# Attention over graph edges: the drops' product as four of 32 columns before the messages, factors first in ScalarE's turn

## What is computed

```python
def gatv2_layer(x, Ws, bs, Wd, bd, attn, src, dst):
    hs = (x @ Ws + bs).reshape(N, H, HD)
    hd = (x @ Wd + bd).reshape(N, H, HD)
    hs_e = hs[src]
    e = jax.nn.leaky_relu(hs_e + hd[dst], SLOPE)
    logits = jnp.einsum('ehd,hd->eh', e, attn)
    m = jax.ops.segment_max(logits, dst, num_segments=N)
    ex = jnp.exp(logits - m[dst])
    s = jax.ops.segment_sum(ex, dst, num_segments=N)
    alpha = ex / s[dst]
    out = jax.ops.segment_sum(alpha[..., None] * hs_e, dst, num_segments=N)
    return jax.nn.elu(out).reshape(N, DM)
```

## Time and profile before

| what | value |
|---|---|
| median of 3 runs | 2284.72 us (2283.73 to 2286.36) |
| span of the profiled execution | 2282.6 us |
| granted TensorE clock, mean | 0.974 of full speed |
| TensorE products | 2141.9 us, 94% |
| TensorE weight loads | 1718.3 us, 75% |
| VectorE | 1671.1 us, 73% |
| ScalarE | 1120.7 us, 49% |
| GpSimd | 770.2 us, 34% |

### The profile page before, as it was taken

The page is one execution under the profiler, slowest core; times in us unless marked ns, Lnnn a source line. Parts: engine busy times, 40 slices in busy tenths (PEclk is TensorE's granted clock), DMA queues, the critical chain, the costliest instruction groups (busy, mean ns, idle before and its releaser), DMA issues. The chain is left out here.

```text
span 2282.6 us, 91572 instructions
## 1 busy us (share of the span) xinstructions
PE 2141.9 (94%) x32341; PEld 1718.3 (75%) x32342; DVE 1671.1 (73%) x4413; ACT 1120.7 (49%) x2757; POOL 770.2 (34%) x798
## 2 busy tenths in 40 slices
PE   5999999998999999999996899899999999999578
PEld 3665555555899999999995556589999999999467
DVE  5224997343888888888887674488888888888873
ACT  1101210023666666666664324466666666666463
POOL 0000001111555555555552001255555555554000
PEclk9999999999999999999998899999999999999789
DMA  5000224333788888888874024488888888887301
GB/s 190 0 1 11 76 97 101 106 121 86 239 251 250 252 250 248 247 256 252 251 249 135 23 85 131 131 244 252 251 249 252 251 252 251 250 249 225 133 22 47
DMA packets 139236, 397.61 MB, mean 174 GB/s; under 512 B 21704, under 2 KB 76267, under 8 KB 139123
## 3 DMA queue, kind: packets, MB, share of 16 engines
q0 software_dynamic: 59584, 298.64, 43.0%
q1 hardware_dynamic: 76525, 90.41, 12.6%
q10 hardware_dynamic: 3044, 7.45, 1.1%
HBM read 368.18 MB, written 16.78 MB: 169 GB/s over the span
## 5 line engine op out<-in xcount | busy, mean ns | idle before, releaser
L498 ACT ACTIVATE at_relu<-at_turned,ah_attn_size 128x512 f32<-128x512 f32 x1092 | 717.9, 694 | 432.0 <-PE at_turned L557 430.6
L479 POOL DMA_INDIRECT at_rows<-table,ah_index x360 | 361.3, 1004 | 295.3 <-DVE ah_index L681 104.1
L479 POOL DMA_INDIRECT ah_room<-table,ah_index x352 | 351.5, 998 | 291.1 <-DVE ah_index L681 122.4
L555 PE MATMUL at_turned<-ah_place,dst_rows 96*128 96x128 bf16 x2208 | 401.1, 223 | 19.3 <-ACTq L533 9.6
L557 PE MATMUL at_turned<-ident,ah_room 128*128 128x128 f32 x2208 | 416.4, 279 | 0.0
L557 PE MATMUL at_turned<-ident,at_rows 128*128 128x128 f32 x2160 | 403.6, 277 | 0.5 <-issue 0.4
L555 PE MATMUL at_turned<-at_place,dst_rows 96*128 96x128 bf16 x2160 | 388.9, 222 | 0.0
L677 DVE SCALAR_TENSOR_TENSOR sums<-sums,at_factor,at_total 128x97 f32 x1456 | 344.0, 310 | 9.0 <-issue 5.1
L557 PEld LDWEIGHTS at_turned<-ident,ah_room 128*128 128x128 f32 x2208 | 317.7, 144 | 24.8
L557 PEld LDWEIGHTS at_turned<-ident,at_rows 128*128 128x128 f32 x2160 | 308.0, 143 | 23.2 <-issue 0.6
L667 DVE TENSOR_TENSOR at_spread<-at_lined,at_weight 128x1024 f32<-128x1024 f32 x182 | 223.0, 1225 | 131.4 <-ACT at_weight L508 118.0
(11 more groups left out here) (318 smaller groups left out, 3195.8 us busy)
## 6 DMA issues: line engine op xcount, KB each, us to landing
at_flags<-run_flags SPq DMA_DIRECT2D x182, 64.0 KB
dst_rows<-pr_parts SPq DMA_DIRECT2D x76, 144.0 KB, 2.5
ah_place<-local_rows SPq DMA_DIRECT2D x92, 96.0 KB
at_place<-local_rows SPq DMA_DIRECT2D x90, 96.0 KB
table<-ah_room SPq DMA_DIRECT2D x20, 400.0 KB, 2.4
ah_room<-table,ah_index POOLq DMA_INDIRECT x368
at_rows<-table,ah_index POOLq DMA_INDIRECT x360
mx_w<-in_L_mix_W_qkv SPq DMA_DIRECT2D x2, 2304.0 KB, 19.3
```

Source lines behind the costliest of these rows:

```text
L479: pool.indirect_dma_start(rows[b][:, j, :], None, table, bass.IndirectOffsetOnAxis(index[b][:, j:j + 1], 0)).then_inc(gathered[b], 16)
L498: act.activation(relu[c][:], turned[chunk(b, c)][:], ACT.Relu, scale=attn_size[:, c:c + 1]).then_inc(bent, 1)
L555: pe.matmul(into, dst_rows[:, bass.ds(at[j], 1), c * P:(c + 1) * P].rearrange("p o d -> p (o d)"), place[b][:, j * P:(j + 1) * P], start=T ...
```

## The change

- `sum_drops` becomes four products of 32 columns instead of one of 128: each takes 32 columns of `head_rows` and writes 32 partitions. The result goes to the bank `back`, behind its first 128 columns, and no longer to `heads`. It now waits for the weights of the macro as well, since they are read from the same bank.
- On TensorE it moves from between chunks 4 and 5 to the front of the next turn, directly before the messages of the same macro.
- On ScalarE `factors` moves from in front of bend 5 to the front of the next turn, which is directly behind bend 5. Both programs get one more turn at the end for it.
- `sum_heads` no longer waits for the factors; the last product into `back` (after the loop) does.

```diff
                 def factors(m, b):
                     act.wait_ge(turned_back, 2 * m + 2)
                     for j in range(G):
-                        act.activation(factor[b % 2][:, j, :], heads[:, P + j * HH:P + (j + 1) * HH], ACT.Exp,
+                        act.activation(factor[b % 2][:, j, :], back[:, P + j * HH:P + (j + 1) * HH], ACT.Exp,
                                        scale=first_dst[:, bass.ds(m * G + j, 1)]).then_inc(weights_ready, 1)
-                def slot(turn, head, first=False, fresh=False):
+                def slot(turn, head, message, first=False):
+                    if message:
+                        factors(message[0], message[1])
                     if turn:
                         bend(turn[0], turn[1], 0, first)
...
                         bend(turn[0], turn[1], 4, first)
-                    if head:
-                        factors(head[0], head[1])
-                    if turn:
                         bend(turn[0], turn[1], 5, first)
...
                 with act.Fori(0, LOOPS) as i:
                     for b in range(UNROLL):
-                        slot(macro(i, b + 2), macro(i, b + 1))
+                        slot(macro(i, b + 2), macro(i, b + 1), macro(i, b))
...
                 def sum_heads(m, b):
                     pe.wait_ge(scanned, m * SCANS + SCANS)
-                    pe.wait_ge(weights_ready, m * EXPS + EXPS)
...
                 def sum_drops(m):
                     pe.wait_ge(dropped, m + 1)
-                    pe.matmul(heads[:, P:P + G * HH], head_rows[:], drop[:], start=True, stop=True).then_inc(turned_back, 1)
+                    pe.wait_ge(weights_ready, m * EXPS + (EXPS + 1))
+                    for q in range(HM):
+                        last = pe.matmul(back[q * S:(q + 1) * S, P:P + G * HH], head_rows[:, q * S:(q + 1) * S], drop[:], start=True, stop=True)
+                    last.then_inc(turned_back, 1)
...
                     if message:
+                        sum_drops(message[0])
                         for pair in range(2):
                             messages(message[0], message[1], pair)
...
-                    if head:
-                        sum_drops(head[0])
                     if turn:
                         turn_chunk(*turn, at, 5)
...
                 pe.wait_ge(merge_ready, 1)
+                pe.wait_ge(weights_ready, NM * EXPS + EXPS)
                 pe.matmul(back[:, 0:2 * G * HH], head_rows[:], gap[:].rearrange("p s k -> p (s k)"), start=True, stop=True).then_inc(merged, 1)
```

More of the change, by code:

```diff
@@ L527, in slot @@
                         bend(turn[0], turn[1], 4, first)
-                    if head:
-                        factors(head[0], head[1])
-                    if turn:
                         bend(turn[0], turn[1], 5, first)
                 act.sem_inc(bent, BANKS)
-                slot(macro(0, 0), None, first=True)
-                slot(macro(0, 1), macro(0, 0))
+                slot(macro(0, 0), None, None, first=True)
+                slot(macro(0, 1), macro(0, 0), None)
                 with act.Fori(0, LOOPS) as i:
                     for b in range(UNROLL):
-                        slot(macro(i, b + 2), macro(i, b + 1))
-                slot(macro(LOOPS, 2), macro(LOOPS, 1))
-                slot(None, macro(LOOPS, 2))
+                        slot(macro(i, b + 2), macro(i, b + 1), macro(i, b))
+                slot(macro(LOOPS, 2), macro(LOOPS, 1), macro(LOOPS, 0))
+                slot(None, macro(LOOPS, 2), macro(LOOPS, 1))
+                slot(None, None, macro(LOOPS, 2))
                 act.wait_ge(merged, 1)
```

## The result

| | before | after |
|---|---|---|
| median (lowest to highest), timed side by side | 2285.54 us (2283.73 to 2287.12) | 2309.78 us (2306.43 to 2315.54) |
| ratio | | 1.0109 [1.0092, 1.0126] |
| span of the profiled execution | 2282.6 us | 2304.6 us |

A forecast was written before the change was run, and what follows sets the result against it. TensorE was taken to pace three turns in four, the loop's jump adding 0.27 us to the fourth. Turns of 7.76, 7.045, 7.33 and 7.30 sum to 29.43 against 28.77, +30 us over 182 turns: 2315 us, range 2292 to 2330.

The forecast's parts named there:

- The circle: Loop turn held by late factors: chunks 3 to 5, bend 5, factors, additions, shift, chunk 3 again; 7.30 us against 7.125.
- The mis-sized term: On TensorE, chunk 3's load to chunk 5's end: 2.50 us less 0.14 for the removed products, 2.36.
- The second turn: Second turn after the loop's jump: the shift ends 4.74 us into it, and it takes 7.33 us.
- The milder rival: Circle of 7.2 us, from `turn_back` starting sooner or a shorter step from `bend` 5 to factors; 2290 to 2302, chance 0.10.
- The jump: Turn at the loop's jump, every fourth: later shift and one more register step make it 7.76 us against 7.39.
- The products: Drops' products in front of the messages on TensorE: removing one saves 0.14 us, the four added take 0.06.
- the sign that was named: On TensorE, first load of the drops' products to first message load: 0.06 us; 0.18 would mean that term was mis-sized.
- TensorE's own turn: Loop turn paced by TensorE alone: from 7.125 to 7.045 us, 0.08 saved, between 0.11 and -0.04.
- the rival on short passes: Drops' products cost more than they save, factors not late: 0.04 us a turn lost, 2296 us; chance 0.03.
- The signs named beforehand: Additions idle about 0.4 us a turn, `turn_back` idle two turns in four, message starts 7.3 apart, 7.75 at the jump.
- The sum: Both loops: four turns take 29.43 us against 28.77, +0.66, which is +30 us over 182 turns.

The follow-up runs named there:

- after: The changed kernel as first measured and profiled beside the kernel before: 2309.78 us, ratio 1.0109.
- order_only_2: The kernel before with only ScalarE's factors moved behind bend 5, run where the kernel before takes 2285.55 us: 2319.35 us, ratio 1.0151.
- wait_last: The changed kernel with the first addition's wait for the factors put behind its wait for `added`, on the slower chip: 2605.45 us, 1.0147 of the kernel before.
- own_factor_2: The changed kernel with each tile's additions waiting only for that tile's factor, run where the kernel before takes 2285.55 us: 2288.26 us, ratio 1.001.
- spread_wait: own_factor_2 with the drops' products waiting for `spread_ready` and `added` instead of `dropped` and `weights_ready`: 2282.52 us, 0.9991 of the kernel before.
- the second set: Follow-up runs timed on a chip where the kernel before takes 2285.55 us: after_again 2310.74, order_only_2 2319.35, own_factor_2 2288.26, spread_wait 2282.52 us.
- after_again: The changed kernel run again, unaltered, where the kernel before takes 2285.55 us: 2310.74 us, ratio 1.0118.
- twice: spread_wait with the four drops' products of 32 columns done two times, on the slower chip: 2591.58 us, 1.0213 of the kernel before.
- whole_product: spread_wait with one drops' product of 128 columns at the same place instead of four of 32, on the slower chip: 2526.69 us, 0.9952 of the kernel before.
- before_own_factor: The kernel before with each tile's additions waiting only for that tile's factor, on the slower chip: 2561.88 us, 0.9976 of the kernel before.
- order_only: The kernel before with only ScalarE's factors moved behind bend 5, on the slower chip: 2534.99 us, 0.9876 of the kernel before.
- own_factor: The changed kernel with each tile's additions waiting only for that tile's factor, on the slower chip: 2595.58 us, 1.011 of the kernel before.
- load_later: spread_wait with TensorE's load of the turn's block numbers moved from the turn's front to behind the messages, on the slower chip: 2514.98 us, 0.9903 of the kernel before.

## Why the prediction was right

**The circle** was right in its links. For a turn that the factors hold, forecast and measured (means over the loops of the changed kernel): chunk 5's end to `bend` 5 0.03 and 0.04 to 0.05; `bend` 5 to the first factor 0.57 and 0.57 to 0.59; the factors 0.74 and 0.71 to 0.74; to the first addition 0.24 and 0.243; to the end of the shift 3.13 and 3.14. That the factors' wait isn't the last step before the addition, read from L674's step after a jump, is in nearly every turn of `after` and of `order_only_2` as 0.24 us between the end of the factors and the addition, and `wait_last` took one of the two steps out of it. `order_only_2` makes the loss with ScalarE's order alone, and `own_factor_2` takes it away with the wait alone.

**The mis-sized term** is the first link, chunk 3's load to the end of chunk 5: forecast 2.36, measured 2.26. I had added it to the 0.23 from the shift to chunk 3's load, which measured 0.237: that term had no row behind it, only bounds, and coming out so near was in part luck. But in the earlier trace rows the load at 729.34 comes 0.11 before its product since the array is still busy with what stands ahead; behind a wait there is nothing ahead. The timeline of TensorE's products and loads in the turn above:

```profile
744.12 0.28 PE L557 MATMUL at_turned<-ident,ah_room 128*128 128x128 f32 x1
744.23 0.30 PE L578 MATMUL at_back<-ident,at_shifted 128*128 128x128 f32 x1
744.40 0.23 PE L555 MATMUL at_turned<-ah_place,dst_rows 96*128 96x128 bf16 x1
```

```profile
744.21 0.14 PEld L578 LDWEIGHTS at_back<-ident,at_shifted 128*128 128x128 f32 x1
744.39 0.10 PEld L555 LDWEIGHTS at_turned<-ah_place,dst_rows 96*128 x1
```

Load and product of chunk 3 (L555) stand 0.01 us apart. With the links as measured the circle is 7.22 rather than 7.30, and that is what the third turn takes. The second turn starts from TensorE's own 7.065, in which chunk 3 didn't stand behind a wait, and takes 7.316 to the forecast 7.33. Its second part was right by two errors that cancel: from the shift to the end of chunk 5 it takes 0.09 us less than forecast, but the messages start 0.085 us behind that end, where the forecast let them start at it. The milder rival (a circle of 7.2, 2290 to 2302) had this value of the circle, but let it hold all the turns; it holds one in four.

**The jump** came out as 7.722, forecast 7.76: the shift ends 4.63 us after the messages' start (forecast 4.71, as if the messages started at chunk 5's end and not 0.085 us behind it), and the messages follow it by 3.09 (forecast 3.05: 2.95 and one register step of 0.1). In `own_factor_2` and `spread_wait` the jump's turn takes 7.563 and 7.515 against 7.377: the messages follow the shift by 3.09 and 3.04 rather than 2.95, and the shift itself ends 0.05 later after the messages' start than it did. In the turn behind the jump the factors also wait for the late products, 0.26 us more (0.845 rather than 0.586 from `bend` 5 to the first factor); as forecast, TensorE's own 7.065 covers it.

**The products** were put at 0.06 us where 0.03 to 0.18 was the range. By the sign that was named, from the first load of L584 to the first message's load, it is 0.057 where TensorE is busy. The turn pays more: the first message product follows its load by 0.029 rather than 0.002, so that from the first load to it there are 0.086 us. Where the sequencer is late it is 0.13, since the messages' own threshold step (L590) now lies between the two; `spread_wait`, which has no such step there, has 0.086 at the jump too. TensorE's own turn is 7.065 to the forecast 7.045, a gain of 0.06 and not 0.08. For the rival on short passes 0.20 us was reckoned by the 25 ns floor of the Trainium skill (TensorE: Matmul & The Clock Gate, "Wait — 56ns, not 53.3ns?"); eight passes take 0.086, 11 ns each, and a further eight 0.063, 8 ns each, so the traces don't agree for passes that write different quarters.

**The signs named beforehand.** Idle of the additions released by factors: there, but smaller than the 0.4 us a turn: 34.6 us over 182 turns is 0.19 a turn, and in the three held turns it is 0.14, 0.32 and 0.16. `bend` 5 behind chunk 5: there, by 0.04 us. Starts about 7.3 apart and 7.75 at the jump: 7.32, 7.22 and 7.72. `turn_back` idle, released by the shift: not in the rows, because the modelled end of the transpose ahead of it (744.12 + 0.28) covers the gap. The distances show it: the load of `turn_back` comes 744.21 - 739.53 = 4.68 after the first message where it was 729.23 - 724.64 = 4.59, 0.06 after the shift's end, and chunk 3's load 0.18 behind it rather than 0.11. Against the first turn, in medians of layer 0, `turn_back`'s load comes 0.10 later after the messages' start and chunk 3's load 0.075 later still; from there to chunk 5's end it takes 0.09 less, and the next messages stand 0.07 further behind that end. Together that is the 0.155 by which this turn exceeds 7.065.

**The sum:** 26 us in the loops to the forecast 30; the circle's 0.08 us are most of the difference. The medians differ by 24.2 us here and by 25.2 in the second set. The profiled execution of `after` was the fastest of its four, 3 us under their median, so that its 4 us elsewhere are best read as differences between executions; that `after_again` doesn't show them fits.

## What to carry to other kernels

A result that no engine waits for today has a cover that can be read off the timeline, here 0.59 us for the factors; moving its maker behind one more operation of 0.57 us spends it, and what the waiting engine still does after the wait (0.24 us here, of which each register step is 0.10) counts too. A late result sets the turn only where its chain closes on itself within it, so follow it round until it meets its start, and at every link ask whether the duration was read where an engine was busy or where it stood waiting. Where one wait covers several results made one by one, waiting for each just before its use can give the cover back: 22 of 25 us here, for three more waits.

## What the runs showed of the hardware

- Products of 32 weight columns that write different quarters run together. With 8 moving columns the four passes of a group start 6 to 7 ns apart in `spread_wait`, and the second group 0.053 us after the first; eight passes take 0.086 us up to the first message, sixteen 0.149 in `twice`, and two passes of 128 weight columns 0.320 in `whole_product`. Both forms load 256 weight columns in all, so their number alone doesn't set the time.
- On VectorE a further wait against a register value costs 0.10 us if it stands behind the wait that ends last: 0.243 us from the factors to the addition with two steps, 0.146 with one (`after`, `wait_last`). Behind such a wait a product of TensorE follows its load by 0.007 us, where in a busy stretch the load is 0.107 us ahead.
- The same program takes 2285 us on one chip and 2540 to 2567 on another, at a mean granted clock of 0.97 on both. In the loop of layer 0 of `before_own_factor`, which is 128.5 us longer than before, the clock is 1.00 as before and TensorE has 77 us more of busy time by the profile. DMA moves 202 GB/s rather than 243, which is the same number of bytes in the longer time. Over the whole program the loads of the messages and of the sums over heads stand idle with no releaser but "issue" for 208 us, as shown above:

```profile
589.60:1366.30 776.70, 716.92 (x13903) 602.43 (x13902) 581.22 (x1616) 444.23 (x1170) 400.62 (x348) 1.00 0.69 202
```

- On that chip the ratio goes in part with the length of TensorE's program in the loop (its products as written and the register steps of the trace): 581 in `before_own_factor`, `order_only`, `whole_product` and the kernel before itself (0.9976, 0.9876, 0.9952, 1), 597 in `own_factor` and `wait_last` (1.011, 1.0147), 609 in `twice` (1.0213). `load_later` breaks the row: 593 with 0.9903. The expectation of `after_again` spoke of TensorE waiting for instructions and of 12 more passes a turn to fetch; there are 6 more passes, each with a load, 12 instructions. That fetching the instructions is what is slow there was only argued; no run took it apart.
